# GpSimd's fill of the key stacks behind the first normalised x; the second batch's key stack in two lanes of one transfer each; w1 and w2 in 8 pieces with two under way

## The reference

```python
x = x + cross_attention(layernorm(x), ctx, ctx)   # ctx: 2 x 2048 x 128, 16 heads of 8
x = x + self_attention(layernorm(x))              # rotary positions, ALiBi bias
x = x + experts(layernorm(x))                     # 16 experts, hidden 512, the best 4 are mixed

# inside cross_attention
scores = einsum('bhqd,bhkd->bhqk', Qh, Kh) / sqrt(8)
scores = clip(scores - max(scores), -1e9, 1e9)
attn = softmax(scores); attn = clip(attn, 1e-12, None)
attn = attn / sum(attn)
```

## Time and profile before

| | us |
|---|---|
| median of 3 runs (301.94 to 302.82) | 302.19 |
| the profiled execution | 302.97 |
| its span, first to last instruction | 300.7 |
| TensorE busy | 207.3 |
| VectorE busy | 173.8 |
| ScalarE busy | 133.1 |
| GpSimd busy | 50.2 |

### The profile page before, as it was taken

The page is one execution under the profiler, slowest core; times in us unless marked ns, Lnnn a source line. Parts: engine busy times, 40 slices in busy tenths (PEclk is TensorE's granted clock), DMA queues, the critical chain, the costliest instruction groups (busy, mean ns, idle before and its releaser), DMA issues.

```text
span 300.7 us, 5478 instructions
## 1 busy us (share of the span) xinstructions
PE 207.3 (69%) x2267; PEld 128.8 (43%) x2267; DVE 173.8 (58%) x274; ACT 133.1 (44%) x280; POOL 50.2 (17%) x53
## 2 busy tenths in 40 slices
PE   0528764601974550888988957788588699999995
PEld 0114550400442220444544534334247477777774
DVE  2789956601995260499999923674855843222242
ACT  1107710100784250489888866433340744444420
POOL 7792340299430000000000000000000000000000
PEclk9999955655798595599999999956557999999999
DMA  6404999858978988810000009400000000000000
GB/s 148 193 0 109 203 161 157 101 102 153 163 87 105 111 78 93 336 72 2 4 3 2 2 3 378 183 3 0 0 2 0 1 2 0 0 0 2 0 0 17
DMA packets 7585, 22.40 MB, mean 74 GB/s; under 512 B 1224, under 2 KB 3880, under 8 KB 6248
## 3 DMA queue, kind: packets, MB, share of 16 engines
q1 hardware_dynamic: 6904, 21.24, 35.5%
q0 software_dynamic: 656, 0.81, 1.6%
HBM read 18.37 MB, written 3.67 MB: 73 GB/s over the span
## 4 chain that ended last, share of the span: by engine, by line
PE 37%; DVE 29%; DMA 14%; issue 11%; ACT 3%; SPq 3%; POOL 1%; POOLq 0%; DVEq 0%; ACTq 0%
DVE mx L482 15%; DMA kst<-parts_d 11%; PE ps L1252 10%; PE ps L1235 8%; PE ps L996 5%; DVE xn L406 4%; PE ps L975 3%; PE ps L946 2%; PE ps L1122 2%; PE ps L1128 2%; DMA ident<-in_ident 2%; DMA parts_d<-w1s 2%; SPq L283 1%; PE ps L1246 1%; ACT ex L805 1%
## 5 line engine op out<-in xcount | busy, mean ns | idle before, releaser
L482 DVE TENSOR_REDUCE mx<-ps 128x2 f32<-128x1024 f32 x64 | 74.5, 1219 | 47.1 <-PE ps L946 47.0
L805 ACT ACTIVATE ex<-ps 128x512 f32<-128x512 f32 x128 | 70.1, 595 | 35.9 <-PE ps L975 34.4
L996 PE MATMUL ps<-ex,vau 128*9 128x128 f32 x1024 | 43.2, 285 | 21.3 <-issue 20.0
L946 PE MATMUL ps<-kst,qst 64*128 64x512 bf16 x128 | 28.0, 437 | 28.2 <-DMA kst<-parts_d 19.5
L704 DVE TENSOR_TENSOR cT<-cT,ps 128x1024 f32<-128x1024 f32 x16 | 19.5, 1221 | 35.2 <-PE ps L1246 33.5
L996 PEld LDWEIGHTS ps<-ex,vau 128*9 128x9 f32 x1024 | 22.4, 92 | 39.2 <-issue 25.8
L847 ACT ACTIVATE cT<-ps,b1s 128x256 f32<-128x256 f32 x64 | 25.9, 474 | 28.8 <-PE ps L1235 28.7
L1252 PE MATMUL ps<-cT,kst 128*128 128x256 f32 x128 | 31.6, 391 | 0.0
L975 PE MATMUL ps<-qst,kst 64*128 64x128 bf16 x512 | 26.8, 227 | 3.2 <-ACT ex L805 2.9
L1235 PE MATMUL ps<-xT,w1s 128*128 128x256 f32 x112 | 26.7, 381 | 2.3 <-ACT cT L847 2.3
L329 POOL TENSOR_TENSOR rstd<-rstd,expo 128x1 f32<-128x1 f32 (+1 forms) x5 | 3.0, 590 | 146.2 <-DVE rstd L400 146.2
(11 more groups left out here) (197 smaller groups left out, 229.0 us busy)
## 6 DMA issues: line engine op xcount, KB each, us to landing
w1s<-in_w SPq DMA_DIRECT2D x4, 1024.0 KB, 43.5
kst<-in_w SPq DMA_DIRECT2D x4, 1024.0 KB, 9.0
parts_d<-w1s SPq DMA_DIRECT2D x8, 384.0 KB, 15.0
cT<-in_ctxT SPq DMA_DIRECT2D x3, 512.0 KB, 6.3
kst<-parts_d SPq DMA_DIRECT2D x2, 768.0 KB
kst<-parts_d SPq DMA_DIRECT2D x2, 576.0 KB
kst<-parts_d SPq DMA_DIRECT2D x2, 512.0 KB
kst<-parts_d SPq DMA_DIRECT2D x4, 192.0 KB
```

The costliest lines, as they stand in the source:

```text
L482: dve.tensor_reduce(out=mx2[:, b, 2 * pair:2 * pair + 2, f], in_=ps[:, bank:bank + 2, :], axis=AX.X, op=ALU.max).then_inc(s["redA"], 1)
L805: act.activation(ex[:, e % NE, :], ps[:, 4 + e % 3, :], ACT.Exp, scale=SCALE).then_inc(s["exp"], 1)
L946: last = pe.matmul(ps[:, bank + a, :], qst[half, pair, a, b * S:(b + 1) * S], kst[half, b, pair, 512 * f:512 * f + 512], start=True, stop= ...
L996: last = pe.matmul(ps[32 * j:32 * j + DK + 1, 7, 128 * hg:128 * hg + 128], vau[:, NK * b + c, GH * hg + j, :], ex[:, (2 * t + j % 2) % NE, ...
```

## The change

Three edits. `ones(0)` is no longer ahead of `rstds(0)`: GpSimd first waits for `xn` and then runs all four fills. The third entry of `STACKS` is gone; in its place SP reads the whole stack of batch 1 by itself, the three transfers of each half in a lane with its own semaphore (`d_k1`): a transfer is issued when the one ahead of it in its lane has landed. `w1` and `w2` go in 8 pieces of half the size (`N_W`) with two semaphores each in turn: a piece is issued when the one two ahead of it has landed; and `w1` waits for both lanes of the stack. TensorE waits for the two lanes instead of one semaphore, at unit 32, ahead of `up` and ahead of `down`.

```diff
-STACKS = [(0, 0, 2), (0, 2, PAIRS), (1, 0, PAIRS)]
+STACKS = [(0, 0, 2), (0, 2, PAIRS)]
...
-            stack(2)
+            sp.wait_ge(s["ones"], 2 * B)
+            for n in (2, 3):
+                sp.wait_ge(d_kd[n], 32)
+            for k, (t0, m) in enumerate(K_RUNS):
+                for a in range(2):
+                    if k:
+                        sp.wait_ge(d_k1[a], 16 * k)
+                    r0 = HALF * a + TERM0 + DK * t0
+                    src = parts_d[1, a, 0:m].rearrange("t (d p) n -> (t d) p n", d=DK)
+                    sp.dma_start(kst[r0:r0 + DK * m, 1, :, :], src).then_inc(d_k1[a], 16)
...
-            for n in range(4):
-                sp.dma_start(w1s[:, n * E * F // 4:(n + 1) * E * F // 4], w1[:, n * E * F // 4:(n + 1) * E * F // 4])\
-                    .then_inc(d_wt, 16)
+            for a in range(2):
+                sp.wait_ge(d_k1[a], 16 * len(K_RUNS))
+            for n in range(N_W):
+                if n >= 2:
+                    sp.wait_ge(d_wt[n % 2], 16 * (n // 2))
+                sp.dma_start(w1s[:, n * E * F // N_W:(n + 1) * E * F // N_W], w1[:, n * E * F // N_W:(n + 1) * E * F // N_W])\
+                    .then_inc(d_wt[n % 2], 16)
...
-            for n in range(4):
-                sp.dma_start(w2s[:, 16 * n:16 * n + 16, :], w2[:, 16 * n:16 * n + 16, :]).then_inc(d_w2, 16)
+            for n in range(N_W):
+                if n >= 2:
+                    sp.wait_ge(d_w2[n % 2], 16 * (n // 2))
+                m = E * FC // N_W
+                sp.dma_start(w2s[:, m * n:m * n + m, :], w2[:, m * n:m * n + m, :]).then_inc(d_w2[n % 2], 16)
...
-            ones(0)
             rstds(0)
-            for n in range(1, 2 * B):
+            pool.wait_ge(s["xn"], 1)
+            for n in range(2 * B):
                 ones(n)
```

More of the change, by code:

```diff
@@ L172, in build @@
         ps = es.enter_context(nc.psum_tensor("ps", [128, 8, 512], fp32))
-        d_x, d_w, d_wq, d_wv, d_q, d_wt, d_w2, d_out, d_const, d_bl, d_bv = (sem("d_" + n) for n in (
-            "x", "w", "wq", "wv", "q", "wt", "w2", "out", "const", "bl", "bv"))
+        d_x, d_w, d_wq, d_wv, d_q, d_out, d_const, d_bl, d_bv = (sem("d_" + n) for n in (
+            "x", "w", "wq", "wv", "q", "out", "const", "bl", "bv"))
         d_c0 = sem("d_c00")
@@ L181, in build @@
         d_qd = sem("d_qd")
+        d_k1 = [sem(f"d_k1{a}") for a in range(2)]
+        d_wt, d_w2 = ([sem(f"d_{n}{lane}") for lane in range(2)] for n in ("w1p", "w2p"))
         d_fg, d_fc, d_fs = ([sem(f"d_{n}{b}") for b in range(B)] for n in ("fg", "fc", "fs"))
@@ L217, in build @@
         LEAD = 2
+        N_W = 8
         AHEAD = 4
@@ L942, in unit @@
                         pe.wait_ge(d_kb[i], 32 * len(K_RUNS))
+                if (b, pair, f) == (1, 0, 0):
+                    for a in range(2):
+                        pe.wait_ge(d_k1[a], 16 * len(K_RUNS))
                 slot_free(("unit", u))
@@ L1206, in _ @@
             turn_sums2(1)
-            pe.wait_ge(d_wt, 16 * 4)
+            for lane in range(2):
+                pe.wait_ge(d_wt[lane], 16 * N_W // 2)
             pe.wait_ge(s["xTc"], 4)
@@ L1273, in _ @@
             pe.matmul(ps[:, 6, 0:B * S], b2s[:], wT[:], start=True, stop=False)
-            pe.wait_ge(d_w2, 16 * 4)
+            for lane in range(2):
+                pe.wait_ge(d_w2[lane], 16 * N_W // 2)
             for e in range(E):
```

## The result

| | before | after |
|---|---|---|
| median of 4 runs, us | 302.50 | 278.79 |
| lowest to highest | 301.94 to 303.67 | 276.21 to 279.73 |
| the profiled execution | 302.97 | 279.28 |
| its span | 300.7 | 277.2 |

The change makes the kernel faster: ratio 0.9198, 95% interval 0.9129 to 0.9267, 23.7 us between the medians. The forecast was 292.0 us with a range from 283 to 300.5. The direction was right, but the gain is more than twice the forecast and the time lies outside the range.

What follows compares the result with a forecast made beforehand. TensorE has most work, but DMA and "issue" (instruction fetches behind stack rows) hold the chain. Unit 32 10.9 us earlier plus 0.9 for the clock gives -10.0: 292.0 us forecast, range 283 to 300.5.

Steps and rivals of the forecast that it cites:

- `xn`: First edit, start of the kernel: with the fill moved behind it, `xn` ends at about 10.9 instead of 20.78, 9.9 us earlier.
- The cast behind the fills: First edit: cast of `kr` held to the end of the last `kst` fill, second block of key parts 1.5 us later.
- The first rival: Casts get in between the fills (-5) or are not held (-9.9): 280.6 to 285.5 us in total; chance 0.17.
- The second batch's stack: Second edit, two lanes: issued at 80.5, 30 us of data plus 4 us for gates and landing, landed at about 115.
- the sum of both limited: Stack and `w1` together limited to 106 GB/s, so the stack's 3.15 MB alone takes 30 us.
- what is late next: Stack, at 115, is late next if unit 32 comes between 107 and 120.6; 118 taken, 10.9 us earlier than the trace.
- The rival in which the stack is as slow as today: A row needs its 5 us whatever runs beside it: stack at 126, -2.9 + 0.9, 299.4 us in total; chance 0.20.
- The idle times: TensorE's "issue" stretches ahead of unit 32: first stays 8.1 us, second shrinks from 11.9 to 3, gaining 8.9 us.
- The rival in which both stay: Slower: fetch stands behind 32 KB rows, both idle times stay (19.9 us), unit 32 at 130.4, total 303.7 us; chance 0.10.
- `w1` and `w2`: Third edit, 8 pieces with two under way: worth nothing on the path; `w1` there at 138, wanted at 226 or later.
- The clock: If TensorE waits at unit 32, its clock is down after it: plus 0.9 us.

## Why the prediction was wrong, step by step

**`xn`: right.** It ends at 10.8, by the forecast 10.9.

**The cast behind the fills: the step that failed.** The prediction took "that the cast is held like `xn`" and put +1.5 us; measured are -8.4. Its reason, that `xn` was held over two borders, was a true reading of the trace, but it took for a property of fills what was one of a power and fills queued without a wait. The changed kernel brings a wait just there, and the prediction did not ask whether the added wait changes how the engines take turns. The first rival had the mechanism and, with -5 to -9.9, the size between its two cases: -5 for one border was too little, since a cast comes 2.5 us into a fill of 3.5 and then waits for 0.84 us only. The sentence on the Trainium skill (SBUF — State Buffer, section "SBUF: two separate sides") set the rule that the shared ports are locked for one instruction against the rows of before. The changed kernel follows the rule, the kernel before does not, and the runs with added waits on GpSimd turn the one into the other. What the same section states on operations with two SBUF inputs, that they meet only a GpSimd operation that reads SBUF, agrees too: the subtraction at L458 takes its usual 1.22 us from 14.97 on, inside the second fill (14.33 to 18.39).

**The second batch's stack: the time roughly right, its part wrong.** By the forecast 34.5 us from the first issue to the last landing, measured 30.0. But the reasoning behind it ("the sum of both limited") does not hold: without `w1`, but at once, it took 36.9 us. Fewer rows under way are faster rows: 3.3 us each in the lanes against 4.3 at once. It was then named as what is late next, for 118 us; unit 32 came at 103.59 and the stack was there 3 us before. The rival in which the stack is as slow as today is refuted; its sum was off as well, since -2.9 + 0.9 from 302.19 gives 300.2 and not 299.4.

**The idle times: mis-sized.** The prediction let the first stay at 8.1 and the second shrink to 3; they are 3.28 and nothing, 16.7 us of gain instead of 8.9. It kept the first whole, because the two transfers of 24 rows are as deep on an engine as before; measured it fell by 4.8 us with the other four transfers not queued behind them. That those four are the reason is argued: with all six queued and `w1` away it was 9.71, with one transfer under way it was gone. That these idle times come from late instruction fetches was right: each ends 1.4 to 2.4 us behind the landing of a packet of instructions, and they come and go with what is queued on the DMA engines while the products that TensorE runs stay the same. The rival in which both stay is refuted.

The prediction's reading of the Trainium skill here (DMA: Bandwidth & Descriptors, section "Queues, rings and completion order") went too far. The section has an engine switch queues behind a packet of typically 9 to 17 descriptors; "one row of 32 KB at most" is not in it. So the 15 us without a fetch do not contradict the section, and no run here shows how many rows an engine took before it turned to the fetch.

**`w1` and `w2`: right.** Their pieces land after 4.4 and 4.3 us, the last of `w1` by about 119, over 80 us before it is wanted (203.5). The lanes alone gave the same time.

**The clock: not foreseen where it came.** The forecast charged 0.9 us for a cold clock behind unit 32, where there was no wait and none came. It came at 148 to 168 us, 1.8 us in the sum with the stretch behind. Why the clock was lower there is open. The runs of the same kernel differ by as much: 276.21 us at a mean granted clock of 0.876, 279.73 at 0.840.

Both sizes erred to the same side: 9.9 us in the first edit and 7.8 in the second, more than the 13.5 us between the forecast -10.0 and the measured -23.5. Nearly all of the rest is in the small terms, to the other side: 2.6 us for the stack that was to be late and 0.9 for a warmer clock did not come, and the clock cost 1.8 instead of 0.9. The range was too narrow at its low end because it put half the chance on one reading of one row.

## What to carry to other kernels

When one engine is idle for many microseconds without a wait and its long program is unrolled, look at the instruction queue among the DMA queues, and whether the engine goes on right behind one of its packets. If so, keep few and small transfers under way while it runs: here two, each waiting for one ahead of it, beat six and one. Before taking a hold between VectorE and GpSimd for a fixed cost, look at what is queued on GpSimd without a wait: one semaphore wait can part it. And when an edit adds a wait, ask what else the wait changes besides the order.

## What the runs showed of the hardware

- Behind a power and three fills on GpSimd that were queued without a wait, an operation on VectorE was held over two borders between fills: 10.62 us for the two operations of `xn` instead of 0.60, 10.56 for a cast instead of 0.23. With one wait behind the power, or one behind each fill, it was let in at the first border: 2.43 and 3.57 us for both operations of `xn`.
- The second batch's stack, 3.15 MB in pieces of 32 KB, took 36.9 us with six transfers at once (and in another order), 30.0 with two under way and 40.5 with one. One piece took 4.3, 3.3 and 2.7 us. In pieces of 16 KB with two under way the stack took 28.9.
- TensorE stood idle for 8 to 12 us behind such transfers, and went on 1.4 to 2.4 us after a packet of 16 KB had landed in the queue "instruction", in all 26 cases. With half the size at once it stood idle for 11.1 and 4.8 us, so the size alone does not set it. What exactly a fetch waits for on its engine stays open, and so does why lanes for the first batch's stack doubled the idle time later on (6.8 against 3.3 us).
